# Output matmuls of the experts that wait relu by relu, and a program block that ends without the drain of GpSimd

## The reference

```
x = x + attention_a(layernorm(x))     # 16 heads of 8, cosine scores
x = x + experts(layernorm(x))
x = x + attention_b(layernorm(x))     # 16 heads of 64, relative position bias
x = x + experts(layernorm(x))
```

```
h          = relu(expert_in @ w1 + b1)     # per expert 384 x 128 by 128 x 512
expert_out = h @ w2 + b2                   # per expert 384 x 512 by 512 x 128
y          = sum over a token's two experts of gate * expert_out
```

## Time and profile before

| | us |
|---|---|
| median of three runs | 1417.54 |
| the profiled execution's own time | 1409.33 |
| its span, first to last instruction | 1407.6 |
| attention_a and routing, up to the first expert's turn | about 382 |
| experts f = 0, first turn to last landing | 382 to 444 |
| attention_b and routing | 444 to about 1326 |
| experts f = 1 to the end of the program | 1328 to 1407.6 |

### The profile page before, as it was taken

How to read it: one execution, slowest core, us unless ns; L and a number is a source line. 1 busy time by engine, 2 the same in 40 slices (tenths; PEclk the granted TensorE clock), 3 DMA queues, 4 the chain that set the end, 5 groups by cost and what they waited for, 6 DMA issues and landing times. The chain is left out here.

```text
span 1407.6 us, 22606 instructions
## 1 busy us (share of the span) xinstructions
PE 1252.3 (89%) x6739; PEld 642.7 (46%) x6739; DVE 937.7 (67%) x2837; ACT 873.8 (62%) x1716; POOL 512.5 (36%) x788
## 2 busy tenths in 40 slices
PE   2899999999396899999999999999999999997492
PEld 1333344333273344544544644544544544545271
DVE  5346656654212787798798798799798798785110
ACT  1799988898041766666666576577567567662040
POOL 2000323224464233233443433433533533434255
PEclk7799999999698999999999999999999999999696
DMA  5564444336953466576676576567576666678222
GB/s 155 128 211 147 134 141 142 132 128 205 198 73 59 105 142 145 142 170 145 145 173 155 134 169 164 132 166 162 131 168 148 136 162 141 141 162 217 70 23 22
DMA packets 132936, 197.91 MB, mean 141 GB/s; under 512 B 35166, under 2 KB 76077, under 8 KB 132816
## 3 DMA queue, kind: packets, MB, share of 16 engines
q1 hardware_dynamic: 104848, 138.67, 38.6%
q0 software_dynamic: 27392, 56.76, 19.3%
q10 hardware_dynamic: 576, 1.05, 0.2%
HBM read 61.75 MB, written 39.24 MB: 72 GB/s over the span
## 5 line engine op out<-in xcount | busy, mean ns | idle before, releaser
L1694 ACT ACTIVATE tile<-tile,low 128x512 f32<-128x512 f32 x512 | 363.5, 714 | 239.3 <-DVE low L1780 239.1
L1470 POOL DMA_DIRECT2D crossed<-blocks x512 | 254.0, 504 | 478.8 <-DVE blocks L1793 436.1
L1780 DVE CUSTOM_DVE_ANT_0 tile<-s_ps,bias 128x512 f32<-128x512 f32 x512 | 330.6, 682 | 41.8 <-PE s_ps L1557 34.8
L681 ACT ACTIVATE probs_a<-score_ps,gbound 128x1024 f32<-128x1024 f32 x256 | 272.2, 1114 | 53.8 <-PE score_ps L962 53.5
L1557 PE MATMUL s_ps<-kT,qT 64*128 64x512 f32 x1024 | 260.1, 619 | 15.1 <-DVE low L1780 13.4
L1793 DVE STREAM_TRANSPOSE blocks<-tile 128x512 f32<-128x512 f32 x384 | 256.8, 694 | 0.0
L1577 PE MATMUL o_psb<-crossed,v_b 128*64 128x512 f32 x512 | 235.6, 603 | 10.0 <-DMA crossed<-blocks 8.9
L389 POOL DMA_INDIRECT slots<-rows_r,slot_r x128 | 128.1, 1001 | 65.7 <-issue 50.6
L1557 PEld LDWEIGHTS s_ps<-kT,qT 64*128 64x128 f32 x1024 | 85.2, 185 | 134.0 <-issue 85.6
L962 PE MATMUL score_ps<-q_stack,k_stack 32*128 32x512 f32 x512 | 123.3, 503 | 18.4 <-DMA q_stack<-q_parts 14.0
L975 PE MATMUL o_ps<-probs_a,v_ext 128*32 128x512 f32 x1024 | 136.8, 608 | 1.3 <-DVE o_sb L794 1.3
(11 more groups left out here) (188 smaller groups left out, 1647.7 us busy)
## 6 DMA issues: line engine op xcount, KB each, us to landing
crossed<-blocks SPq DMA_DIRECT2D x512, 96.0 KB
crossed<-blocks POOLq DMA_DIRECT2D x512, 96.0 KB
inv_row<-inv_rows SPq DMA_DIRECT2D x128, 128.0 KB, 4.4
q_parts<-parts SPq DMA_DIRECT2D x32, 256.0 KB, 3.8
k_stack<-k_parts SPq DMA_DIRECT2D x32, 256.0 KB, 3.4
q_stack<-q_parts SPq DMA_DIRECT2D x32, 256.0 KB, 4.3
w_f<-in_w SPq DMA_DIRECT2D x32, 256.0 KB, 5.9
k_parts<-parts SPq DMA_DIRECT2D x28, 256.0 KB, 3.6
```

Of the source, the lines that this page charges most:

```text
L681: nc.scalar.activation(probs[q % 2][:, c % 4 // 2, pair:pair + 2, :].rearrange("p h t -> p (h t)"), score_ps[c % 2][:, :], ACT.Exp, bias=g ...
L1470: pool.dma_start(strip_to(n, a, m), strip_from(n, a, m)).then_inc(crossed_sw[n % 2], 16)
L1694: nc.scalar.activation(tile[(b * NS + k) % RING][s][:, :], tile[(b * NS + k) % RING][s][:, :], ACT.Exp, bias=low[n % 2][:, s, i:i + 1], sc ...
L1780: nc.vector.tensor_tensor_reduce(out=tile[(b * NS + k) % RING][s][:, :], in0=s_ps[k % 2][s][:, :], in1=bias[:, h, off:off + S], scale=1.0, ...
```

## The change

Two edits. First, the one wait of PE for all four relus is replaced by four: in the first token tile (c = 0) the matmul of piece m waits for the m-th relu alone. The matmuls of the tiles c = 1 and 2 have no wait of their own. The wait for ob_ready (an O_ps tile that is free again) stays, but now stands ahead of the waits for h_ready. Second, the block is opened with `no_gpsimd_drain=True`.

```diff
@@ experts, block.tensor @@
                 if e + 1 < E_N:
                     turn(e + 1)
-                pe.wait_ge(h_ready, (e + 1) * HC)
                 if e >= 2:
                     pe.wait_ge(ob_ready, e - 1)
                 for c in range(CT):
                     for m in range(HC):
+                        if c == 0:
+                            pe.wait_ge(h_ready, e * HC + m + 1)
                         last = nc.tensor.matmul(out_of(e, c), hT[e % 2][:, m, c * P:(c + 1) * P],
                                                 w2[:, e, m, :], start=(m == 0), stop=(m == HC - 1))
@@ build @@
-        block = ctx.enter_context(nc.Block())
+        block = ctx.enter_context(nc.Block(no_gpsimd_drain=True))
```

## The result

The changed kernel takes 1407.24 us in the median of 20 runs (1397.47 to 1411.51), the kernel before 1411.05 us in 20 runs beside it (1406.66 to 1421.01). The ratio is 0.9955, with a 95% interval from 0.9936 to 0.9975: 0.45% faster, 6.3 us by the means and 3.8 us by the medians. The forecast was 8.8 us or 0.62%. It stood on three runs of before, whose median of 1417.54 lies 6.5 us above that of the 20. These three are among the 20; the other 17 have a mean 5.2 us above that of the changed kernel.

The account below looks back on a forecast made before the run. PE was taken to bound f = 0, POOL and its DMAs f = 1, and POOL's DRAIN the end. Gains of 4.2 + 0.6 + 4.0 = 8.8 us gave 1417.54 - 8.8 = 1408.7 us, range 1405.0 to 1414.5.

Parts of the forecast that it names:

- The waits: First expert layer (f = 0): splitting PE's wait saves 0.60 us per expert, 4.2 us over seven, so attention_b starts earlier.
- satisfied waits cost nothing: Output matmuls on PE: three more per expert carry a wait, costed at nothing; the bound was 0.10 us each.
- f = 1: Second expert layer: POOL's first group comes 0.6 us earlier; later groups stay 7.96 us apart, so experts 1 to 7 give nothing.
- The drain: End of the program: without POOL's DRAIN, signals follow the branch directly, 4.0 us less in the span.
- the first rival: End of the program: the drain only moves behind the span, so gain 4.8 us and time 1412.7; chance 0.22.
- none of the terms is in these: Own time's 1.7 us over the span and the median's 8.2 us over own time stay, so 8.8 us carries over whole.
- a rival of 0.04: Attention_b, starting 4.2 us earlier, meets the lower clock; at 30 us of it the time is 1423.7; chance 0.04.
- theory P: From the experiments: PE's stall some 35 us into attention_b falls at a worse moment, so the clock falls behind it.

Follow-up runs that it names:

- pair_both: The changed kernel with both edits, against the kernel before on the same chip: 8.6 us below it, ratio 0.994.
- its twin: The changed kernel plus two matmuls without use in PE's stall some 35 us into attention_b, against the kernel before: 8.1 us below, ratio 0.9938.
- shifted and filled kernels: Changed kernel plus 0.86 us useless work before expert 3's transposes (f = 0), or two useless matmuls in attention_b's stall: 8.6 and 8.2 us below before.
- both_bridge: Changed kernel, two useless matmuls in attention_b's stall, ten more ahead of attention_b, eight for four at its start, against before: 10.3 us below, ratio 0.9931.

## Why the prediction was right and wrong

**The waits, right in the trace.** Period 5.60 forecast, 5.59 measured; POOL's gap 0.38 and 0.36; POOL from first to last DMA 3.6 us shorter, which is 6 x 0.60. That satisfied waits cost nothing held: 24 output matmuls in 2.84 us, where they took 2.94 with the stall's refilling. The profiled attention_b starts 5.6 us earlier and not 4.2, since the clock rose earlier during the first expert's hidden layer (4.26 us and not 5.42).

**f = 1, right for the first group and wrong for what follows.** In the two profiles the stretch from the first transpose to POOL's first DMA went from 12.07 to 11.71 us, and by 0.65 in the mean of the traces. The groups stay bound by landings, but they were forecast to stay 7.96 us apart, and the second came up to 1.7 us later.

**The drain, right.** 4.0 us of the span, and no run shows it come back: time minus span stayed 1.72 us. That refutes the first rival here. The page "VectorE: DVE Perf Modes" of the Trainium skill, section "The DRAIN you can't avoid", states drains of the runtime of about 12 ns on all engines. That one of them would take over the removed one's 4 us was my inference, and no run here shows it. In the means of the runs the drain alone was worth 2.3 and 4.7 us.

**The step that failed** is the one from the stages to the whole: "none of the terms is in these", with all that stands behind a shortened stage taken to last as long as before. The missing term is 8.8 - 6.4 = 2.4 us (error 0.7). The traces have 0.8 (0.25) of it in POOL's groups with f = 1, where the first landing comes later, and 1.4 (0.8) in attention_b. The first was put at nothing without a reason. For the second the clock was kept as a rival of 0.04, with the argument that the idle time ahead has the same length and no fall is in 822 us. Neither holds: PE's idle time grew from 8.79 to 9.43 us, and a fall of 3.4 us lay just ahead of these 822 us.

What causes the two losses stays open. That the missing 2.4 us go with a lower granted clock is shown by the runs; that the fall behind the stall at 36 us takes them (theory P) is not borne out, as the stages' lengths and pair_both with its twin stand against it. The shifted and filled kernels gained 2.2 and 1.8 us more (errors about 1.2 and 1.0), each at less than two errors, and the traces don't show why. One limit is that unshifted traces with the old waits come from three of the six series only. In these three the new waits lengthen the last row of the table in two and not in the third.

**The base was off too.** The median of the first three runs, 1417.54, lies 6 to 10 us above every later median of the same kernel (1407.6 to 1411.1). So the forecast time of 1408.7 us came within 1.5 us of the measured median by luck: the base was 6.5 us too high, and the gain by the medians 5 us too small.

## What to carry to other kernels

A wait for a group of results can be split at no cost where the first consumers need only one each; look at which engine is next in line, and count only what its slack takes. A stage that starts earlier doesn't have to last as long: before you add up a gain of under 1%, compare the length of every later stage, and the mean clock, over several executions. Measure such a length from the start of the stage and not from one stall on, or a loss that another execution had earlier looks like one that only this execution has. A mean clock also counts idle time that costs nothing.

## What the runs showed of the hardware

GpSimd's DRAIN lasted 4.0 us in the closing section, though its last visible work had ended 1.9 us before, and without it the kernel ends 0.4 us behind the branch that waits for the last landing. In one trace (both_bridge) ten matmuls without use kept TensorE at its upper clock level across what was an idle time of 9.4 us; in the kernels without them it ran at the lower level for the first 2 to 6 us of the next stage. One kernel's executions differ in where the clock falls: in the first 50 us of attention_b, past those first us, it was at the lower level for 0, 3.4, 6.8 or 10.2 us in the traces. The landing of a first group of three indirect DMAs came up to 1.7 us later in the 11 of 20 traces in which a packet of the instruction queue started 5 us or more behind the first of them.
